# Feed-forward stage moved into the attentions' block: its first body runs among the attention's last products, its weights are rounded in six pieces, its buffers are lent

## The chip, the cores and the metric

One core of a Trainium2 chip runs the whole layer as one program. The metric is the device time of that program in microseconds (us); smaller is better. TensorE (PE) multiplies, VectorE (DVE) and ScalarE (ACT) work on tiles, GpSimd (POOL) does small vector work, SyncE (SP) issues the transfers. Each engine runs its own instructions in the order in which they are written; engines meet through semaphores.

## The reference, cut to what matters

Tokens are x of 32 batches by 64 positions by 256 features.

```python
x = x + attention1(mixture_of_experts(x, cond))          # 8 experts, top 2
def cond2(x, t):                                          # t is cond_256
    x = x + _attention(_tc_rmsnorm(x, t, g1w, g1b, b1w, b1b), Wq, Wk, Wv, Wo)
    return x + _swiglu(_tc_rmsnorm(x, t, g2w, g2b, b2w, b2b), gate_w, hid_w, out_w)
def _tc_rmsnorm(x, t, gw, gb, bw, bb):
    g = (t @ gw.T + gb)[:, None, :]; b = (t @ bw.T + bb)[:, None, :]
    return g * x * jax.lax.rsqrt(jnp.mean(x * x, axis=-1, keepdims=True) + 1e-6) + b
def _swiglu(x, gate_w, hid_w, out_w):                     # hidden width 1024
    return jax.nn.silu(x @ gate_w.T) * (x @ hid_w.T) @ out_w.T
x = x + slot_ffn(cond2(x, cond))                          # 16 slots with an expert each
```

The change concerns the second attention (`_attention` above) and `_swiglu`.

## The kernel before, in words

The program is a row of stages: `route`, `experts` with `routed_experts`, `attention` (both attentions, one after the other), `swiglu`, `slots` and the rest. A stage with its own `nc.Block()` ends in a barrier of all engines, and its semaphores are cleared there. `routed_experts` and `attention` share one block ("mid"), so attention starts while the last expert tiles finish. `swiglu` has its own block.

Tokens lie as 16 tiles of 128 (TT = 16), and work goes by bodies of two tiles, 256 tokens (NBODY = 8). `attention` runs the first attention's bodies 0 to 7 (tiles t = 0 to 15), then the second's (j = 0 to 7, t = 16 to 31), in an order written out by hand for each engine. A body of the second attention has `keys`, `queries` and `values` (12 matmuls of 256 columns each, since each product is made of three with operands split in a rounded high and a low part, `mm3`), and for each of its two tiles `scores`, `turn_weights` and `results`; `turn_results` and `project_results` of the body before are put between. On DVE a tile's `softmax` is a maximum and a subtraction over 1024 columns; `masked` writes the keys `kx` three times under a mask (`scores` of the next body waits for it); ACT does `exps`, the copies out of PSUM (`keys`, `queries`, `weights`, `results_turned`) and `squares` (the sums of squares for the next norm). The input of a body goes: `scaled` on ACT, `turn` on PE, `adapt` on DVE, `biased` on POOL, `high` on ACT, `low` on DVE.

The feed-forward stage's weights, 3 MB, are fetched into `g.w_ff` by SP in one transfer after the first attention's tile 0 (L805), in front of the transfers that the later bodies need (`results_in`, `load`). In `swiglu`, ACT takes a square root of all tokens' norms, rounds each of three weights whole (`wh`, 128x2048) and DVE makes the low parts (`wl`). Then eight bodies run, each with four steps j: `pair` (12 matmuls into pG, 12 into pH), ACT `silu` of pG, DVE `gated` (product with pH), ACT `hidden_high`, DVE low part, PE `output` (12 matmuls into pO). Body i's first `pair` goes ahead of the last `output` of body i - 1. Bodies 2 to 5 are a loop of two bodies' code, run twice. Beside these, `turn_key_weights`, `slot_queries`, `stationary`, `slot_scores_of_features` and `fold_high`/`fold_low` prepare folded weights for `slots`. SP stores `g.x1` to memory and loads weights of a later stage into `g.w_small` and `g.x1` (`lent_down`, `lent_up`).

Of the kernel before, what the change touches and what calls it, by code (L numbers as in the profile page):

```python
# [646 lines left out]

HD1 = DH + 1
# [52 lines left out]
def attention(nc, g, dr, block, sem):  # L701
    with ExitStack() as ctx:
# [8 lines left out]
        gat = [[sb(f"gat{c}{n}", [P, 2, D]) for n in range(2)] for c in range(2)]  # L711
        ya = [sb(f"ya{a}", [P, D]) for a in range(2)]
        yt = [sb(f"yt{a}", [P, D]) for a in range(2)]
        vst = [sb(f"vst{a}", [P, 4, 8, 2, HD1]) for a in range(2)]
        condT = sb("condT", [DC, NB])
        adaw = sb("adaw", [DC, 4, D])
        adab = sb("adab", [P, 4, KD])
        wh = [sb(f"wh{n}", [P, KD, D], F32R) for n in range(4)]
        wl = [sb(f"wl{n}", [P, KD, D], F32R) for n in range(4)]
        wo = sb("wo", [P, KD, D])  # L720
        neg = sb("neg", [P, 2])
        rows = [sb(f"rows{a}", [P, 2, D]) for a in range(2)]
        rT = sb("rT", [P, KD, PB])
        xb = [sb(f"xb{a}", [P, 2, D]) for a in range(2)]
        junk = [sb(f"junk{a}", [P, D]) for a in range(2)]
        xT = sb("xT", [P, KD, PB])
        kT = sb("kT", [P, KD, PB])
        m4 = sb("m4", [P, HR])
        warm = sb("warm", [P, HR])
# [6 lines left out]
        ol = sb("ol", [P, KD, PB], F32R)  # L736
        mx = [sb(f"mx{a}", [P, NH]) for a in range(2)]
# [3 lines left out]
        rs = [sb(f"rs{n}", [P, TT]) for n in range(4)]  # L741

# [6 lines left out]
        pR = pA[:, 0:NH * HD1].rearrange("p (h d) -> p h d", h=NH)  # L749
        pa = pD[:, 0:4 * KD * NB].rearrange("p (n k b) -> p n k b", n=4, k=KD)  # L750
# [8 lines left out]
        ada_in, ada_ps, ada_sb, ff_in, wo_in, neg_ok, rs_ok, inv_ok = (  # L759
            sem(n) for n in ("ada_in", "ada_ps", "ada_sb", "ff_in", "wo_in", "neg_ok", "rs_ok", "inv_ok"))  # L760
        wh_ok, wl_ok, u1_ok, u2_ok, uh_ok, ul_ok, q_ps, q_sb, ot_ps, oh_ok, ol_ok, o2_ps, o2_sb = (
            sem(n) for n in ("wh_ok", "wl_ok", "u1_ok", "u2_ok", "uh_ok", "ul_ok", "q_ps", "q_sb", "ot_ps", "oh_ok", "ol_ok", "o2_ps", "o2_sb"))
        o_out = [sem(f"o_out{a}") for a in range(2)]
# [6 lines left out]
        def _(sp):  # L770
# [42 lines left out]
        def _(pool):  # L813
# [25 lines left out]
            def biased(j):  # L839
                pool.wait_ge(u1_ok, j + 1)  # L840
                if j > 0:
                    pool.wait_ge(ul_ok, j)
                nc.gpsimd.tensor_tensor(batches(u2[:, :, :]), batches(u1[:, :, :]), bc(g.ada[:, 1, :, 4 * j:4 * j + 4], 3, S), ALU.add).then_inc(u2_ok, 1)
# [22 lines left out]
            for j in range(NBODY):  # L866
                if j < 4:
                    root(j + 4)
                if j + 2 < NBODY:
                    biased(j + 2)  # L870

        @block.tensor
        def _(pe):
            def turn(b):
# [4 lines left out]
                if b > NBODY:  # L879
                    pe.wait_ge(k_sb, 2 * b)  # L880
                    pe.wait_ge(u1_ok, b - NBODY)
# [136 lines left out]

            pe.wait_ge(ada_in, 48)
# [54 lines left out]
            for j in range(NBODY):  # L1074
                t = TT + 2 * j
                scores(t + 1)
                if j + 1 < NBODY:
                    keys(j + 1)
                turn_weights(t)
                if j + 1 < NBODY:  # L1080
                    queries(j + 1)
# [5 lines left out]
                if j + 1 < NBODY:  # L1087
                    scores(t + 2)
                if j + 2 < NBODY:
                    turn(NBODY + j + 2)  # L1090
# [5 lines left out]
                else:  # L1096
                    if j + 1 < NBODY:
                        values(j + 1)
# [4 lines left out]
            project_results(NBODY - 1)  # L1103

        @block.scalar
        def _(act):
# [15 lines left out]
            def scaled(j):  # L1122
                act.wait_ge(inv_ok, j + 1)
                act.wait_ge(x_ps, NBODY + j)
                for a in range(2):
                    nc.scalar.activation(yt[a][:, :], g.x1[:, 2 * j + a, :], ACT.Copy, scale=g.inv1[:, 2 * j + a:2 * j + a + 1]).then_inc(yt_ok, 1)
# [7 lines left out]
            def high(j):  # L1134
                act.wait_ge(u2_ok, j + 1)
                if j > 0:
                    act.wait_ge(q_ps, j)
                    act.wait_ge(v_ps, NBODY + j)
                nc.scalar.activation(uh[:, :, :], u2[:, :, :], ACT.Copy).then_inc(uh_ok, 1)
# [113 lines left out]
            for j in range(NBODY):  # L1253
                t = TT + 2 * j
                if j + 1 < NBODY:
                    keys(j + 1)
                weights(t)
                if j + 1 < NBODY:
                    queries(j + 1)
                if j > 0:  # L1260
                    results_turned(j - 1)
                if j + 2 < NBODY:
                    scaled(j + 2)
# [6 lines left out]
                if j + 1 < NBODY:  # L1270
                    exps(t + 2)
                    values(NBODY + j + 1)
# [4 lines left out]
            squares(N2 - 3)  # L1277
            squares(N2 - 2)
            results_turned(NBODY - 1)
            squares(N2 - 1)  # L1280

        @block.vector
        def _(dve):
# [15 lines left out]
            def adapt(j):  # L1299
# [3 lines left out]
                v.tensor_tensor(batches(u1[:, :, :]), batches(two(pC)), bc(g.ada[:, 0, :, 4 * j:4 * j + 4], 3, S), ALU.mult).then_inc(u1_ok, 1)  # L1303

            def low(j):
                dve.wait_ge(uh_ok, j + 1)
                v.tensor_tensor(ul[:, :, :], u2[:, :, :], f32(uh[:, :, :]), ALU.subtract).then_inc(ul_ok, 1)
# [83 lines left out]
            for j in range(NBODY):  # L1391
                t = TT + 2 * j
                softmax(t + 1)
                if j + 1 < NBODY:
                    masked(NBODY + j + 1)
# [3 lines left out]
                if j + 1 < NBODY:  # L1399
                    softmax(t + 2)  # L1400
                if j + 2 < NBODY:
                    adapt(j + 2)
                if j < LAG:
# [3 lines left out]
                    if j + 2 < NBODY:  # L1407
                        low(j + 2)
                else:
                    if j + 1 < NBODY:  # L1410
                        values(NBODY + j + 1)
# [9 lines left out]
def self_attention(nc, g, dr, first, w_raw, wo_raw, res, out, ssq):  # L1421
    if not first:
        with g.moe_sems, ExitStack() as ctx:
            _, _, sem = scope(nc, ctx, "mid")
            block = ctx.enter_context(nc.Block())
            routed_experts(nc, g, dr, block, sem)
            attention(nc, g, dr, block, sem)


def project_first(nc, g, dr):  # L1430

    pass


KF = FH // P
MP = KF // 2


def swiglu(nc, g, dr):
# [11 lines left out]
    with ExitStack() as ctx:  # L1451
        sb, ps, sem = scope(nc, ctx, "ffn")
        wh = [sb(f"wh{n}", [P, KD * FH], F32R) for n in range(3)]
        wl = [sb(f"wl{n}", [P, KD * FH], F32R) for n in range(3)]
        ms = sb("ms", [P, TT])
# [1173 lines left out]
```

## Time and profile before

| | |
|---|---|
| time, median of 3 runs | 962.15 us (956.14 to 964.59) |
| the profiled execution's own time | 968.49 us |
| its span, first to last instruction | 966.3 us |
| mean granted TensorE clock | 0.929 |
| busy: PE / DVE / ACT / POOL | 87% / 61% / 56% / 20% |
| PE's first feed-forward matmul | 597.75 us |
| last feed-forward result | 739.60 us |

All times of rows count from the span's start. The profiled execution is one run, 6.3 us over the median; differences worked out in it are carried over to the median.

### The profile page before, as it was taken

The numbers are of one execution on the slowest core, as the hardware profiler recorded it, in microseconds if no ns is written. First come the engines' busy times: TensorE is split into PE (matmuls) and PEld (weight loads), VectorE is DVE, ScalarE is ACT, GpSimd is POOL, SyncE is SP. The second block draws the span as 40 slices with busy tenths as digits, with TensorE's granted clock in tenths as the row PEclk, the third lists the DMA queues.
The fourth block names the chain that finished last, engine by engine and source line by source line (L and its number), as shares of the span: only waits on it lengthen the run. The fifth ranks groups of instructions, "written<-read, shape, count | busy, mean of one in ns | idle before, by whom it ended". The sixth has DMA issues, their size and how long they took to land. (4 is left out here: it accounts for less than half of the span.)

```text
span 966.3 us, 21254 instructions
## 1 busy us (share of the span) xinstructions
PE 839.9 (87%) x8416; PEld 729.8 (76%) x8416; DVE 585.5 (61%) x916; ACT 540.1 (56%) x990; POOL 198.0 (20%) x208
## 2 busy tenths in 40 slices
PE   6339989999999978899999985999998975977797
PEld 4239989999999975677778875999998973433354
DVE  3737766777777638788668754454443765321196
ACT  3219877888888735577576655433332541432364
POOL 0032444444354222235221000000000000000052
PEclk8559999999999999999999985999999996997899
DMA  8153666666666424542100005000002933999321
GB/s 327 45 218 125 220 224 215 239 246 233 232 230 230 138 92 144 109 89 45 35 2 1 3 1 218 1 1 1 0 1 106 422 117 165 399 423 425 129 85 67
DMA packets 70374, 145.04 MB, mean 150 GB/s; under 512 B 42648, under 2 KB 48280, under 8 KB 62728
## 3 DMA queue, kind: packets, MB, share of 16 engines
q1 hardware_dynamic: 63504, 127.25, 36.4%
q0 software_dynamic: 5168, 14.36, 4.5%
q10 hardware_dynamic: 1608, 2.12, 0.6%
q8 instruction: 65, 1.06, 0.4%
q14 instruction: 29, 0.24, 0.1%
HBM read 129.29 MB, written 14.42 MB: 149 GB/s over the span
## 5 line engine op out<-in xcount | busy, mean ns | idle before, releaser
L84 PE MATMUL moe_pH<-moe_hh,moew_wh 128*128 128x256 f32 x368 | 102.7, 279 | 0.9 <-DVE moe_hl L608 0.9
L85 PE MATMUL moe_pH<-moe_hh,moew_wl 128*128 128x256 f32 x368 | 102.5, 279 | 0.0
L86 PE MATMUL moe_pH<-moe_hl,moew_wh 128*128 128x256 f32 x368 | 102.5, 278 | 0.0
L608 DVE TENSOR_TENSOR moe_hl<-k_w_ff,moe_hh 128x512 fp32r<-128x512 f32 x92 | 63.8, 693 | 59.9 <-ACT moe_hh L570 59.9
L455 POOL DMA_INDIRECT results_of_experts<-k_w_ff,moew_place_of x46 | 67.5, 1468 | 152.0 <-DMA results_of_experts<-k_w_ff,moew_place_of 92.9
L561 ACT ACTIVATE k_w_ff<-moe_pH,moe_b 128x256 f32<-128x256 f32 x184 | 76.9, 469 | 29.2 <-PE moe_pH L86 29.2
L84 PEld LDWEIGHTS moe_pH<-moe_hh,moew_wh 128*128 128x128 f32 x368 | 69.8, 190 | 1.4 <-DVE moe_hl L608 1.1
L85 PEld LDWEIGHTS moe_pH<-moe_hh,moew_wl 128*128 128x128 f32 x368 | 69.1, 188 | 0.0
L86 PEld LDWEIGHTS moe_pH<-moe_hl,moew_wh 128*128 128x128 f32 x368 | 69.1, 188 | 0.0
L463 POOL DMA_INDIRECT k_w_ff<-in_x_tm,moew_row_of x46 | 52.3, 1137 | 73.8 <-POOLq L71 51.3
L570 ACT ACTIVATE moe_hh<-k_w_ff 128x512 fp32r<-128x512 f32 x92 | 58.2, 632 | 2.9
L599 DVE TENSOR_TENSOR moew_wl<-k_x,moew_wh 128x1024 fp32r<-128x1024 f32 x48 | 56.6, 1221 | 4.8 <-ACT moew_wh L546 3.6
L84 PE MATMUL moe_pY<-moew_wh,moe_hh 128*128 128x256 f32 x180 | 52.8, 293 | 1.6 <-DVE moe_hl L608 1.6
L599 DVE TENSOR_TENSOR moew_wl<-moew_raw,moew_wh 128x1024 fp32r<-128x1024 f32 x44 | 52.0, 1222 | 3.0 <-ACT moew_wh L546 2.7
L84 PE MATMUL moe_pH<-moe_xh,moew_wh 128*128 128x256 f32 x184 | 52.2, 284 | 1.5 <-DVE moe_xl L603 1.5
L1808 POOL DMA_DIRECT2D queries_of_tokens<-slots_qT x8 | 4.5, 561 | 235.1 <-ACT slots_qT L1913 235.1
L86 PE MATMUL moe_pH<-moe_xl,moew_wh 128*128 128x256 f32 x184 | 52.1, 283 | 0.0
L85 PE MATMUL moe_pH<-moe_xh,moew_wl 128*128 128x256 f32 x184 | 52.1, 283 | 0.0
L1688 DVE TENSOR_TENSOR ffn_hf<-ffn_pH,ffn_sg 128x512 f32<-128x512 f32 x32 | 22.1, 692 | 48.8 <-PE ffn_pH L86 35.6
L86 PE MATMUL moe_pY<-moew_wl,moe_hh 128*128 128x256 f32 x180 | 51.0, 283 | 0.0
L85 PE MATMUL moe_pY<-moew_wh,moe_hl 128*128 128x256 f32 x180 | 51.0, 283 | 0.0
L546 ACT ACTIVATE moew_wh<-k_x 128x1024 fp32r<-128x1024 f32 x44 | 45.2, 1051 | 8.9 <-PE moe_pY L86 6.2
(389 smaller groups left out, 2605.7 us busy)
## 6 DMA issues: line engine op xcount, KB each, us to landing
ring<-in_w_slot SPq DMA_DIRECT2D x10, 2048.0 KB, 17.5
k_x<-in_w SPq DMA_DIRECT2D x24, 512.0 KB, 6.6
k_x<-in_w SPq DMA_DIRECT2D x12, 1024.0 KB, 6.7
moew_raw<-in_w SPq DMA_DIRECT2D x22, 512.0 KB, 6.1
moew_raw<-in_w SPq DMA_DIRECT2D x11, 1024.0 KB, 6.6
ring<-in_w_slot SPq DMA_DIRECT2D x9, 1024.0 KB, 16.9
k_w_ff<-in_w_slot SPq DMA_DIRECT2D x4, 2048.0 KB, 11.8
attn_gat<-results_of_experts SPq DMA_DIRECT2D x16, 256.0 KB, 3.5
```

The costliest lines, as they stand in the source:

```text
L84: nc.tensor.matmul(out, ah, bh, start=start, stop=False)
L85: nc.tensor.matmul(out, al, bh, start=False, stop=False)
L86: return nc.tensor.matmul(out, ah, bl, start=False, stop=stop)
L455: nc.gpsimd.indirect_dma_start(out=dr.ys, out_offset=bass.IndirectOffsetOnAxis(ap=g.place_of[:, 2 * j + s:2 * j + s + 1], axis=0), in_=ys[ ...
L463: nc.gpsimd.indirect_dma_start(out=xr[j % 2][:, s, :], out_offset=None, in_=x_rows, in_offset=bass.IndirectOffsetOnAxis(ap=g.row_of[:, 2 * ...
L546: nc.scalar.activation(wh[a][l][:, n], raw_w[a][l][:, n], ACT.Copy).then_inc(wh_ok[l], 1)
L561: last = nc.scalar.activation(ht[l][:, 2 * i + m, :], pH[l][i][:, m, :], ACT.Relu, bias=b12[j % 2][:, l * KM + 2 * i + m:l * KM + 2 * i + ...
L570: nc.scalar.activation(hh[l][:, 2 * i:2 * i + 2, :], ht[l][:, 2 * i:2 * i + 2, :], ACT.Copy).then_inc(hh_ok[l], 1)
L599: v.tensor_tensor(wl[a][l][:, n], raw_w[a][l][:, n], f32(wh[a][l][:, n]), ALU.subtract).then_inc(wl_ok[l], 1)
L608: v.tensor_tensor(hl[l][:, s, :], ht[l][:, s, :], f32(hh[l][:, s, :]), ALU.subtract).then_inc(hl_ok[l], 1)
L1688: v.tensor_tensor(hf[j % 2][:, :, :], pH[j % 2][:, :, :], sg[j % 2][:, :, :], ALU.mult).then_inc(hf_ok, 1)
L1808: pool.dma_start(dr.q[i:i + 1].rearrange("o p k n -> p (o k) n"), qT[i % 2][:, :, :]).then_inc(q_out[i % 2], 16)
```

## The change

`swiglu` is emptied and its work put into `attention`, within the block "mid":

- `kx`, `df` and `ex` lie in `g.w_ff` (`lent`), which is therefore not loaded. The weights come in six pieces of 128x1024 (512 KB) into `raw`, two halves of `g.w_small`, during the second attention; SP issues them after the first attention's last output and the store of `g.x1`, each from the third on after the piece two before it is rounded.
- ACT's `feed_high` and DVE's `feed_low` round one piece at the end of each of the second attention's bodies j = 2 to 6, and the sixth in the last one. `feed_low` waits for `feed_high` of the same piece.
- The root of each feed-forward body's norm is taken on POOL (`second_root`, six small operations) and not on ACT.
- Bodies of the input chain run on: `scaled`, `turn`, `adapt`, `biased` (body 0) and `high`, `low` take the indices 8 to 15.
- The last attention body (t = 30, 31) is written out anew, with `gate`, `raised`, `lowered` (the former `pair` and `output`) of feed-forward body 0 between its products. pG and pH are halves of pS, pO is pD, and the split inputs and hidden values lie in `uh`, `ul`, `wh` and `wl`.
- The eight feed-forward bodies are unrolled. `turn_key_weights` moves behind body 0, `slot_scores_of_features` into body 1, the folds into body 2.
- One barrier (between attention and feed-forward) is gone; the one left clears the semaphores of both.

```diff
-        kx = sb("kx", [P, KD, HR, PB])
-        df = [sb(f"df{a}", [P, NH, S]) for a in range(2)]
-        ex = [sb(f"ex{a}", [P, NH, S]) for a in range(2)]
+        lent = g.w_ff[:, :, :].rearrange("p n m -> p (n m)")
+        kx = lent[:, 0:2048].rearrange("p (k r n) -> p k r n", k=KD, r=HR)
+        df = [lent[:, 2048 + 1024 * a:3072 + 1024 * a].rearrange("p (h k) -> p h k", h=NH) for a in range(2)]
+        ex = [lent[:, 4096 + 1024 * a:5120 + 1024 * a].rearrange("p (h k) -> p h k", h=NH) for a in range(2)]
...
+        fh = [sb(f"fh{n}", [P, KD * FH], F32R) for n in range(3)]
+        fl = [sb(f"fl{n}", [P, KD * FH], F32R) for n in range(3)]
+        raw = [g.w_small[:, 2 - 2 * n:4 - 2 * n].rearrange("p w k n -> p (w k n)") for n in range(2)]
+        ih, il = (uh, wh[0]), (ul, wl[0])
+        hh, hl = (wh[1], wh[2]), (wl[1], wl[2])
+        sg = [lent[:, 512 * r:512 * r + 512].rearrange("p (m n) -> p m n", m=2) for r in range(2)]
+        hf = [lent[:, 1024 + 512 * r:1536 + 512 * r].rearrange("p (m n) -> p m n", m=2) for r in range(2)]
...
-                if t == 0:
-                    sp.dma_start(g.w_ff[:, :, :], dr.w_ff).then_inc(ff_in, 16)
                 if t % 2 == 0 and t >= 2:
                     load(t // 2 - 1)
             load(NBODY - 1)
-            sp.wait_ge(ff_in, 16)
+            sp.dma_start(slotT[:, :, :], dr.slotT).then_inc(sl_in, 16)
+            sp.wait_ge(wl_ok, 3)
+            sp.wait_ge(o1_sb, NBODY)
+            sp.dma_start(g.x1_home, g.x1[:, :, :]).then_inc(x1_out, 16)
+            for p in range(6):
+                if p >= 2:
+                    sp.wait_ge(fl_ok, p - 1)
+                sp.dma_start(raw[p % 2], dr.w_ff[:, p // 2, p % 2 * FH:(p % 2 + 1) * FH]).then_inc(raw_in[p % 2], 16)
+            sp.wait_ge(fl_ok, 6)
+            sp.dma_start(g.lent_down[0], dr.w_slot[LENT, :, W2_AT:W_SLOT]).then_inc(g.lent_down_in[0], 16)
...
+            def second_root(i):
+                c = slice(2 * i, 2 * i + 2)
+                pool.wait_ge(sq_ok, 2 * (NBODY + i) + 2)
+                nc.gpsimd.tensor_scalar(ms[:, c], g.ss2[:, c], 1.0 / D, EPS, ALU.mult, ALU.add).then_inc(rs2_ok, 1)
...
+                elif j < NBODY - 1:
+                    second_root(j - 4)
+                if j + 2 <= NBODY:
                     biased(j + 2)
+            for i in range(NBODY - 5, NBODY):
+                second_root(i)
...
+            def gate(i, j):
+                n = MP * i + j
+                if j == 0:
+                    pe.wait_ge(uh_ok, NBODY + i + 1)
+                    pe.wait_ge(ul_ok, NBODY + i + 1)
+                if n == 0:
+                    pe.wait_ge(fh_ok, 2)
+                    pe.wait_ge(fl_ok, 2)
+                if n < 2:
+                    pe.wait_ge(df_ok, 2 * TT - 1)
+                else:
+                    pe.wait_ge(sg_ok, n - 1)
+                features_of(pG[j % 2], 0, i, j).then_inc(g_ps, 1)
...
+            t = 2 * TT - 2
+            scores(t + 1)
+            turn_weights(t)
+            turn_results(NBODY - 2)
+            results(t)
+            gate(0, 0)
+            turn_weights(t + 1)
+            raised(0, 0)
+            results(t + 1)
+            project_results(NBODY - 2)
+            gate(0, 1)
+            raised(0, 1)
             turn_results(NBODY - 1)
+            lowered(0, 0)
             project_results(NBODY - 1)
+            turn(N2 + 1)
+            for j in range(2, MP):
+                gate(0, j)
+                raised(0, j)
+                lowered(0, j - 1)
+            turn_key_weights()
...
+            def feed_high(n, half):
+                act.wait_ge(raw_in[half], 16 * (n + 1))
+                c = slice(half * FH, (half + 1) * FH)
+                nc.scalar.activation(fh[n][:, c], raw[half], ACT.Copy).then_inc(fh_ok, 1)
...
+                if j >= 2:
+                    feed_high((j - 2) // 2, j % 2)
+            high(NBODY)
+            t = 2 * TT - 2
+            weights(t)
+            exps(t + 1)
+            results_turned(NBODY - 2)
+            squares(N2 - LAG - 2)
+            feed_high(2, 1)
+            silu(0, 0)
+            weights(t + 1)
+            squares(N2 - LAG - 1)
+            scaled(NBODY + 1)
+            silu(0, 1)
+            hidden_high(0, 0)
             squares(N2 - 2)
             results_turned(NBODY - 1)
+            hidden_high(0, 1)
+            high(NBODY + 1)
             squares(N2 - 1)
+            for j in range(2, MP):
+                silu(0, j)
+                hidden_high(0, j)
+                if j == 2:
+                    scaled(NBODY + 2)
...
+            def feed_low(n, half):
+                dve.wait_ge(fh_ok, 2 * n + half + 1)
+                c = slice(half * FH, (half + 1) * FH)
+                v.tensor_tensor(fl[n][:, c], raw[half], f32(fh[n][:, c]), ALU.subtract).then_inc(fl_ok, 1)
...
+                if j >= 2:
+                    feed_low((j - 2) // 2, j % 2)
+            t = 2 * TT - 2
+            softmax(t + 1)
+            low(NBODY)
+            results(t)
+            output_low(NBODY - 2)
+            feed_low(2, 1)
+            results(t + 1)
+            second_output(NBODY - 2)
+            gated(0, 0)
             output_low(NBODY - 1)
+            gated_low(0, 0)
+            gated(0, 1)
+            gated_low(0, 1)
             second_output(NBODY - 1)
+            adapt(NBODY + 1)
+            gated(0, 2)
+            gated_low(0, 2)
+            low(NBODY + 1)
+            gated(0, 3)
+            gated_low(0, 3)
```

## Rows read from the trace of the kernel before

**Rows 1.** Windows: busy time and count per engine, PE clock, DMA share, GB/s.

```profile
540.00:560.00 20.00, 19.52 (x252) 17.01 (x244) 15.30 (x26) 14.97 (x33) 1.04 (x1) 1.00 0.01 2
...
580.00:600.00 20.00, 9.10 (x42) 8.55 (x43) 8.45 (x11) 12.67 (x23) 0.00 (x0) 0.56 0.54 208
...
572.00:574.00 2.00, 1.79 (x8) 1.42 (x8) 0.00 (x0) 0.69 (x2) 0.00 (x0) 0.56 0.00 0
```

**Rows 2.** Timeline, attention's end to the slots' start: start, duration, work, idle before, releaser.

```profile
588.36 1.28 ACT L1652 ACT_TABLE_LOAD   x1 [1.65 <-PEq L71]
...
597.75 0.55 PE L84 MATMUL ffn_pG<-ffn_ih,ffn_wh 128*128 128x256 f32 x1 [3.40 <-DVE ffn_il L1680]
...
599.66 1.28 ACT L1619 ACT_TABLE_LOAD   x1
600.96 0.60 ACT L1619 ACTIVATE ffn_sg<-ffn_pG 128x512 f32<-128x512 f32 x1
...
607.42 0.28 PE L1580 MATMUL ffn_pO<-ffn_wl,ffn_hh 128*128 128x256 f32 x1
...
739.60 0.69 DVE L1695 TENSOR_TENSOR k_x<-ffn_pO,k_x 128x512 f32<-128x512 f32 x1 [1.84 <-PE ffn_pO L1580]
...
741.21 0.63 PE L1819 MATMUL slots_pX<-k_ident,k_x 128*128 128x128 f32 x4 [1.65 <-PEq L71]
```

**Rows 3.** Timeline of PE: the score products of the second attention.

```profile
546.62 1.09 PE L665 MATMUL attn_pS<-attn_kx,attn_qT 64*64 64x256 f32 x16
...
553.23 1.09 PE L665 MATMUL attn_pS<-attn_kx,attn_qT 64*64 64x256 f32 x16
...
560.12 1.09 PE L665 MATMUL attn_pS<-attn_kx,attn_qT 64*64 64x256 f32 x16
```

**Rows 4.** Timeline of DVE and ACT in the same body.

```profile
547.79 1.23 DVE L1328 TENSOR_REDUCE attn_mx<-attn_pS 128x16 f32<-128x1024 f32 x1 [0.17 <-PE attn_pS L665]
...
553.92 0.68 DVE L1356 TENSOR_TENSOR k_x<-attn_pB,k_x 128x512 f32<-128x512 f32 x1
...
556.91 1.27 DVE L1314 TENSOR_SCALAR attn_kx<-attn_kT,attn_m 128x512 f32<-128x512 f32 x3
559.80 0.69 DVE L1352 TENSOR_TENSOR attn_ol<-attn_pB,attn_oh 128x512 fp32r<-128x512 f32 x1 [1.62 <-ACT attn_oh L1202]
...
552.02 0.63 ACT L1139 ACTIVATE attn_uh<-attn_u 128x512 fp32r<-128x512 f32 x1 [2.16 <-POOL attn_u L843]
...
555.18 0.19 ACT L1211 ACTIVATION_READ_ACCUMULATOR attn_junk<-k_x 128x1 f32 x1
```

**Rows 5.** The page's costliest groups: busy us, mean ns of one, idle before.

```profile
L599 DVE TENSOR_TENSOR moew_wl<-k_x,moew_wh 128x1024 fp32r<-128x1024 f32 x48 | 56.6, 1221 | 4.8 <-ACT moew_wh L546 3.6
...
L1688 DVE TENSOR_TENSOR ffn_hf<-ffn_pH,ffn_sg 128x512 f32<-128x512 f32 x32 | 22.1, 692 | 48.8 <-PE ffn_pH L86 35.6
...
L546 ACT ACTIVATE moew_wh<-k_x 128x1024 fp32r<-128x1024 f32 x44 | 45.2, 1051 | 8.9 <-PE moe_pY L86 6.2
```

**Rows 6.** Timeline of PE in the last attention body: its waits.

```profile
569.32 0.63 PE L1003 MATMUL attn_pB<-k_ident,attn_otm 128*128 128x128 f32 x4 [0.83 <-ACT attn_pt L1184]
...
572.08 0.94 PE L962 MATMUL attn_pA<-k_ident,attn_ex 128*128 128x128 f32 x4 [1.07 <-DVE attn_otm L1343]
...
582.30 0.39 PE L84 MATMUL attn_pB<-attn_wh,attn_oh 128*128 128x256 f32 x1 [1.52 <-DVE attn_ol L1352]
```

**Rows 7.** First attention: the weights' transfer (KB, us to landing), then PE's timeline.

```profile
k_w_ff<-in_w_ff SPq DMA_DIRECT2D x1, 3072.0 KB, 10.6
...
390.91 0.75 PE L884 MATMUL attn_pC<-k_ident,attn_yt 128*128 128x128 f32 x4 [2.11 <-DVE attn_yt L1297]
391.59 1.99 PE L665 MATMUL attn_pS<-attn_kx,attn_kT 64*64 64x256 f32 x16
...
404.48 0.66 PE L884 MATMUL attn_pC<-k_ident,attn_yt 128*128 128x128 f32 x4
...
416.46 0.66 PE L884 MATMUL attn_pC<-k_ident,attn_yt 128*128 128x128 f32 x4
```

More of the change, by code:

```diff
@@ new lines, in turn_key_weights @@
+            def turn_key_weights():
+                pe.wait_ge(ot_ok, 2 * TT)
+                pe.wait_ge(o2_sb, NBODY)
+                for c in range(KD):
+                    for k in range(KD):
+                        last = nc.tensor.transpose(two(pA)[:, c, k * P:(k + 1) * P], g.w_small[:, W_DK, k, c * P:(c + 1) * P], g.ident[:, :])
+                last.then_inc(wk_ps, 1)
+                pe.wait_ge(sl_in, 16)
+                for m in range(KD):
+                    for k in range(KD):
+                        last = nc.tensor.matmul(pB[:, m * NS:(m + 1) * NS], g.w_small[:, W_DQ, k, m * P:(m + 1) * P], slotT[:, k, :], start=k == 0, stop=k == KD - 1)
+                last.then_inc(sq_ps, 1)
@@ L1073, in _ @@
             values(0)
-            for j in range(NBODY):
+            for j in range(NBODY - 1):
                 t = TT + 2 * j
                 scores(t + 1)
-                if j + 1 < NBODY:
-                    keys(j + 1)
+                keys(j + 1)
                 turn_weights(t)
-                if j + 1 < NBODY:
-                    queries(j + 1)
+                queries(j + 1)
                 if j > 0:
@@ L1096, in _ @@
                 else:
-                    if j + 1 < NBODY:
-                        values(j + 1)
+                    values(j + 1)
                     results(t + 1)
@@ L1398, in _ @@
                 results(t)
[L1399 to L1402, printed above, removed]
+                softmax(t + 2)
+                adapt(j + 2)
                 if j < LAG:
@@ L1416, in _, with kept @@
                     second_output(j - 1)
+                if j >= 2:
[9 more added lines that the diff above has]
+            gated(0, 0)
             output_low(NBODY - 1)
+            gated_low(0, 0)
+            gated(0, 1)
+            gated_low(0, 1)
             second_output(NBODY - 1)
[L1421 to L1439, printed above, removed]
+            adapt(NBODY + 1)
[4 more added lines that the diff above has]
+            gated_low(0, 3)
+            for i in range(1, NBODY):
+                gated(i, 0)
+                gated_low(i, 0)
+                fed(i - 1)
+                if i + 1 < NBODY:
+                    adapt(NBODY + i + 1)
+                gated(i, 1)
+                gated_low(i, 1)
+                if i == 1:
+                    stationary()
+                gated(i, 2)
+                gated_low(i, 2)
+                if i + 1 < NBODY:
+                    low(NBODY + i + 1)
+                gated(i, 3)
+                gated_low(i, 3)
+                if i == 2:
+                    for n in range(3):
+                        fold_low(n)
+            fed(NBODY - 1)
+def kept(nc, g, dr):
     g.more, g.fold = ExitStack(), ExitStack()
@@ L1741, with self_attention, project_first, swiglu @@
+def self_attention(nc, g, dr, first, w_raw, wo_raw, res, out, ssq):
+    if not first:
+        with g.moe_sems, ExitStack() as ctx:
+            _, _, sem = scope(nc, ctx, "mid")
+            block = ctx.enter_context(nc.Block())
+            routed_experts(nc, g, dr, block, sem)
+            kept(nc, g, dr)
+            attention(nc, g, dr, block, sem)
+def project_first(nc, g, dr):
+    pass
+def swiglu(nc, g, dr):
+    pass
 NRING = 4
```

499 lines of the change are left out of this document (198 added, 301 removed).

## The prediction, made before the changed kernel was run

> **What bounds the kernel now.** I read the windows first, to see where each engine is full, then the timelines of the stretch around the change, and last the first attention, because a transfer leaves it. In the second attention PE is full (19.5 of 20 us) while DVE has 15.3 and ACT 15.0; between 580 and 600 us PE has 9.1 us and a clock of 0.56 [rows 1]. A body of the second attention takes 560.12 - 546.62 = 13.50 us [rows 3]: PE sets it. The feed-forward stage is PE's alone as well: from the end of body 0's first `output` at 607.5 to the last result at 739.6 it needs 132.1 us [rows 2] for 1092 of its 1152 large matmuls, 0.121 us each with the small work between. What is not PE's is the joint. The last two attention bodies' products wait on ACT and DVE [rows 6], the clock falls to half at 572 [rows 1], then come the barrier, the table load for the root, the rounding of weights, and the first product starts only at 597.75, still slow (0.55 us against 0.28 later) [rows 2]. The change aims at this joint.
>
> **The change, part by part.** I count from the score product at 553.23 [rows 3], which opens the last body but one's second half, to the last feed-forward result at 739.60 [rows 2]: 186.4 us before. After, this stretch is the following sum.
>
> 1. One full attention body, 13.5 us [rows 3]. Before, this body (j = 6) lacked `turn`, `adapt`, `biased` and `high`; now it has them for feed-forward body 0.
>
> 2. The last body's attention products at full clock, about 9.3 us: 13.5, less `keys`, `queries`, `values` (36 matmuls at 0.121, 4.4), less one score product (1.0) and one `turn` (0.6), plus one more `turn_results` (0.6) and `project_results` (12 x 0.121, 1.5), less the 0.4 us of waits in a body.
>
> 3. The whole feed-forward stage at its own rate: 132.1 x 1152 / 1092 = 139.4 us. Same order of products, same copies, so I keep the rate; the code is unrolled now, as the attention's code is already, where PE shows no wait for instructions. `turn_key_weights` lies inside it now: 0.9 us at full clock.
>
> 4. The pieces. One costs ACT 1.05 and DVE 1.22 us [rows 5]. Both have idle time in a body, but they work in order and this is where I expect the price. `feed_low` is queued on DVE ahead of the next `softmax`, and waits for ACT, which comes to `feed_high` only after `squares`. Behind it on DVE stand `softmax`, `masked` and all else, and for `masked` the next `scores` on PE waits. I follow the ring: DVE's maximum at 547.79 leads by way of `adapt` and POOL to ACT's `high` at 552.02; ACT ends `squares` at 555.4; `feed_high` to 556.3, `feed_low` to 557.5. In the profile the next maximum begins right behind the result of 553.92 + 0.68 and the masks end at 556.91 + 1.27 = 558.2 [rows 4], 3.6 us later; so now they end at 561.1. The score product of 1.09 us follows and the ring closes with the next maximum at 562.4. That is 14.6 us in place of 13.50, and 1.15 us for each piece. Four pieces (j = 2 to 5) delay a following body: 4.6 us. Bounds: nothing, if the slack of rows 4 (DVE 1.62 us) took it; 2.3 us each, if both roundings came in series, 9.2. I take the ring's value since each of its links is a row.
>
> 5. Waits of PE in the last body. `turn_results` waits for ACT's `weights`, which now stand behind `high` and the fifth piece, about 1.0; `gate(0, 0)` waits for DVE's `softmax` of the last tile (late by the fifth piece) and `low`, 1.0; `results` of the last tile waits for `weights`, which ACT does after the sixth piece (1.05), a table load of 1.28 and the first `silu` of 0.60 [rows 2, 5], 1.9; `lowered(0, 0)` waits for `turn_results`, ACT's copy, `output_low` and `gated_low` at 0.69 each [rows 4, 5], 2.1. Sum 6.0. Before, the nearest waits there were 0.83, 1.07 and 1.52 [rows 6], 3.4 together, which is my lower end; the upper is 10, if each grew by another piece. Behind a late `weights` nothing but this same chain stands.
>
> 6. The clock. Waits of about 1 us in this very place were followed by half clock at 572 [rows 1, 6], a wait of 2.11 by two score products' time (1.99 for 1.09) [rows 7]. With gate products between, one dip is likely: half clock for some 4 us costs 2.0. Ends 0 and 5.
>
> 7. The exit. The barrier with the attention's semaphores took 1.65 us, the one after feed-forward 0.9 (740.3 to 741.2) [rows 2]; the larger stands at the end now: 0.7.
>
> Sum: 13.5 + 9.3 + 139.4 + 0.9 + 4.6 + 6.0 + 2.0 + 0.7 = 176.4 us, 10.0 less than 186.4. The root's table load, the three whole roundings and the first barrier are gone in this; they were in front of 597.75 and nothing takes their place, since `second_root` runs on POOL, which has 1 us of work in 20 [rows 1], and a body ahead of its use.
>
> 8. The first attention. The 3 MB transfer takes 10.6 us to land, and `results_in` is queued behind it; PE waits 2.11 us for that input and then runs its score product at 1.99 us. The body from 390.91 to 404.48 is 13.57 us where the next is 11.98 [rows 7]. Without the transfer I take back the part of the wait that the neighbouring body doesn't have, 1.4, and the 1.6 us: 3.0 (0 to 3.7). The pieces come later, when the DMA engines are at 0.01 [rows 1]: six of 512 KB, by the 3 MB in 10.6 us under 3 us each, a body or two ahead of their use. The store of `g.x1` ahead of them (2 MB) has a body as well. `lent_down` and `lent_up` still end a hundred us before `slots`. No cost.
>
> So 13.0 us less. The profiled execution's own 968.49 becomes 955.5; against the median of the runs, 6.3 lower, 962.15 becomes 949.1, and I say 949.
>
> ACT now has three `squares` between `silu`s (in the last attention body), and no row shows whether the two share a table: `squares` between exponentials need no load, a root does (1.28 us) [rows 2]. If not, ACT gets four more loads, 5.1 us, of which those ahead of `results_turned` and the third `silu`, about 2 us, would reach PE.
>
> The Trainium skill, page "ScalarE: Activation LUTs", section "What ACT_TABLE_LOAD costs", has a higher price: about 2.66 us for each switch, drain included. Here `silu` starts 1.30 us after its load begins, so the trace disagrees as far as the wait is seen; by the page the four loads would be 10.6 us. The section "Table sets: the hidden batching unit" of the same page says that cheap functions are in every set as filler, without naming the square.
>
> **The rivals.**
>
> A. The pieces' waits pull down the clock in each body. PE would sit 1 us more before `scores` in five bodies. For it: half clock after the waits of rows 6 and 7. Against it: a body full of large matmuls lies around the wait. The dip after 390.91 cost 1.6 us (step 8), five of them 8.0: 5.0 us faster only, 957.1.
>
> B. Slower than before: the same place, worse. The pieces are in series (2.3 us a body, 1.15 more than I take, 4 times, 4.6) and each of the five bodies has two such dips, 16.0. Then 20.6 - 13.0 is 7.6 us slower, 969.7. It decides from 2.6 us a body on. Against it: in rows 1 PE keeps full clock in this stage.
>
> C. The overlap doesn't come: the last body's chain (scores, exponentials, results, projection) is so stretched by the inserted ACT and DVE work that feed-forward body 0 is only moved around in it. Waits of 10 us and a clock loss of 5 in place of 8 leave 6.0 us, 956.2.
>
> D. Table loads at each `squares`: 2 us less, 951.1.
>
> **How the numbers follow.** A difference within 1% (9.6 us) can hardly be told from none here. Forecast 0.58, A 0.16, B 0.05, C 0.15, D 0.06. The range for 8 in 10 reaches to A and C and to the good ends of steps 4 to 6 (4.6 + 2.6 + 2.0, of which I take most): 941 to 960. Faster by over 1% (below 952.5) is the forecast and D without their upper part: 0.61; slower by over 1% is part of B: 0.04; the rest, 0.35, is within 1%.
>
> **What would show it.** Score products 14.6 us apart from body 3 on, with DVE idle before the low part of a piece on ACT (step 4; 13.5 would mean it is free). Bodies 2 and 3 of the first attention at 11 to 12 us (step 8). First gate product about 6 us after the last score product, and PE waits of 6 us until `lowered(0, 0)` (step 5). Clock 1.0 in the second attention (against A, B). Feed-forward bodies at 17.1 us as before (step 3). One table load around the squares (D). I am wrong if the feed-forward bodies are slower unrolled or if the last attention body costs PE over 16 us of waiting.

## The result and the profile after

The changed kernel takes 956.5 us (median of 20 runs, 947.8 to 965.5); the kernel before took 963.2 us beside it (20 runs). The ratio is 0.992 (0.990 to 0.995): 7.4 us faster, give or take 2.5, where I had forecast 13.0. That is under 1%, but the interval does not reach 1, so the change is faster by a little. The ratio is formed over all fast executions, so its 7.4 us are not the 6.7 between the medians. The changed kernel's profiled execution took 956.16 us, span 954.3, clock 0.946. The one before took 968.49, 5 us over its own median and slower than 19 of the 20 timed runs, so the two profiles differ by 12.3 us and not by 7.4. That alone warns against reading one against the other to the microsecond.

Windows of the changed kernel, as [rows 1]:

```profile
540.00:560.00 20.00, 17.99 (x233) 15.95 (x231) 15.59 (x23) 15.43 (x31) 6.24 (x13) 1.00 0.18 53
560.00:580.00 20.00, 16.16 (x219) 14.10 (x216) 14.39 (x24) 15.58 (x33) 7.05 (x15) 1.00 0.13 40
580.00:600.00 20.00, 17.94 (x154) 17.73 (x153) 9.39 (x15) 7.59 (x19) 4.96 (x17) 1.00 0.32 122
```

The hole of [rows 1] is gone: between 580 and 600 us PE has 17.9 us of work at a clock of 1.00, where it had 9.1 at 0.56. But the attention's bodies, which had PE at 19.5 of 20, now have 18.0. PE's timeline shows the score products, as [rows 3], and then every wait of the last body, as [rows 6]:

```profile
546.31 1.09 PE L667 MATMUL attn_pS<-k_w_ff,attn_qT 64*64 64x256 f32 x16 [0.77 <-issue]
...
552.86 1.09 PE L667 MATMUL attn_pS<-k_w_ff,attn_qT 64*64 64x256 f32 x16
...
560.92 1.09 PE L667 MATMUL attn_pS<-k_w_ff,attn_qT 64*64 64x256 f32 x16 [0.76 <-issue]
...
567.47 1.10 PE L667 MATMUL attn_pS<-k_w_ff,attn_qT 64*64 64x256 f32 x16
...
570.42 0.63 PE L1055 MATMUL attn_pB<-k_ident,attn_otm 128*128 128x128 f32 x4 [0.83 <-ACT attn_pt L1380]
...
572.71 0.36 PE L84 MATMUL attn_pS<-attn_uh,attn_fh 128*128 128x256 f32 x1 [0.60 <-issue]
...
578.27 1.13 PE L690 MATMUL attn_pA<-attn_vst,attn_pt 128*64 128x34 f32 x32 [1.65 <-ACT attn_pt L1380]
...
586.33 0.36 PE L1121 MATMUL attn_pD<-attn_fh,attn_wh 128*128 128x256 f32 x1 [2.06 <-issue]
```

A body now takes 560.92 - 546.31 = 14.61 us instead of 13.50. The waits sum to 0.83 + 0.60 + 1.65 + 2.06 = 5.14 us. The ring of the piece, on ACT and DVE, as [rows 4]:

```profile
554.94 1.04 ACT L1309 ACTIVATE attn_fh<-k_w_small 128x1024 fp32r<-128x1024 f32 x1
...
553.60 0.68 DVE L1620 TENSOR_TENSOR k_x<-attn_pB,k_x 128x512 f32<-128x512 f32 x1
556.01 1.23 DVE L1543 TENSOR_TENSOR attn_fl<-k_w_small,attn_fh 128x1024 fp32r<-128x1024 f32 x1 [1.74 <-ACT attn_fh L1309]
557.16 1.22 DVE L1592 TENSOR_REDUCE attn_mx<-attn_pS 128x16 f32<-128x1024 f32 x1
...
559.55 1.27 DVE L1578 TENSOR_SCALAR k_w_ff<-attn_kT,attn_m 128x512 f32<-128x512 f32 x3
```

DVE stands idle 1.74 us for `feed_high`, and the maximum of the next tile, whose product had long been done, begins only behind `feed_low`. The masks end at 560.82 and the score product starts at 560.92. The end of the stage, as [rows 2], and ACT's only table load in the joint:

```profile
575.35 1.28 ACT L1316 ACT_TABLE_LOAD   x1
576.64 0.60 ACT L1316 ACTIVATE k_w_ff<-attn_pS 128x512 f32<-128x512 f32 x1
577.13 0.59 ACT L1380 ACTIVATE attn_pt<-attn_pA 128x512 f32<-128x512 f32 x1
...
578.09 0.43 ACT L1407 ACTIVATE attn_junk<-k_x 128x256 f32<-128x256 f32 x1
```

```profile
724.74 0.69 DVE L1561 TENSOR_TENSOR k_x<-attn_pD,k_x 128x512 f32<-128x512 f32 x1 [1.82 <-PE attn_pD L1123]
...
727.46 0.63 PE L1832 MATMUL slots_pX<-k_ident,k_x 128*128 128x128 f32 x4 [2.76 <-PEq L71]
```

The weights for `turn_weights` of the last tile (577.13) stand behind the load and the first `silu`. The squares at 578.09 follow a `silu` without another load. Last, the first attention, as [rows 7]:

```profile
375.83 0.66 PE L936 MATMUL attn_pC<-k_ident,attn_yt 128*128 128x128 f32 x4 [0.57 <-DVE attn_yt L1522]
376.42 1.99 PE L667 MATMUL attn_pS<-k_w_ff,attn_kT 64*64 64x256 f32 x16
...
388.99 0.66 PE L936 MATMUL attn_pC<-k_ident,attn_yt 128*128 128x128 f32 x4 [0.60 <-DVE attn_yt L1522]
389.58 1.09 PE L667 MATMUL attn_pS<-k_w_ff,attn_kT 64*64 64x256 f32 x16
```

The wait of 2.11 us is down to 0.60. The slow score product (1.99 us) is still there, a body earlier; in both repeats of this kernel below it is not (see step 8).

### The profile page after: what moved, and what is told of

It reads as the page before. It is cut to its first block and busy times, and to the rows that moved or that the text cites. A ratio compares the mean times of both kernels' runs of the same rounds, so it can differ in the third digit from the quotient of the medians.

```text
span 954.3 us, 21191 instructions
## 1 busy us (share of the span) xinstructions
PE 837.6 (88%) x8416; PEld 728.9 (76%) x8416; DVE 584.2 (61%) x916; ACT 537.7 (56%) x991; POOL 214.8 (23%) x257
## 5 line engine op out<-in xcount | busy, mean ns | idle before, releaser
L463 POOL DMA_INDIRECT k_w_ff<-in_x_tm,moew_row_of x46 | 48.5, 1053 | 76.2 <-POOLq L71 53.9
L1551 DVE TENSOR_TENSOR k_w_ff<-attn_pS,k_w_ff 128x512 f32<-128x512 f32 x32 | 22.1, 691 | 50.4 <-PE attn_pS L86 34.6
L546 ACT ACTIVATE moew_wh<-moew_raw 128x1024 fp32r<-128x1024 f32 x44 | 45.1, 1051 | 6.4 <-DMA moew_raw<-in_w 3.9
```

The lines of the kernel that those rows point to most:

```text
L463: nc.gpsimd.indirect_dma_start(out=xr[j % 2][:, s, :], out_offset=None, in_=x_rows, in_offset=bass.IndirectOffsetOnAxis(ap=g.row_of[:, 2 * ...
L546: nc.scalar.activation(wh[a][l][:, n], raw_w[a][l][:, n], ACT.Copy).then_inc(wh_ok[l], 1)
L1551: v.tensor_tensor(hf[j % 2], pH[j % 2], sg[j % 2], ALU.mult).then_inc(hf_ok, 1)
```

## The experiments

All were timed against the kernel before on their own chip. Beside each median stands a length read from the profile: from the start of the score product of tile 23 (508.99 in the changed kernel, just ahead of the first body that a piece delays) to the end of the last `lowered` matmul. It holds all delays by pieces, the joint and the whole feed-forward stage, and leaves out the other stages, whose time varies in unaltered code too: the first and the third profile of the changed kernel have spans of 954.3 and 946.2 us, and this stretch takes 215.7 in both.

| kernel | median us | ratio to before (95%) | stretch us |
|---|---|---|---|
| before | 963 to 966 | 1 | 226.8 |
| e4_before_late_ff | 961.4 | 0.998 (0.995 to 1.001) | 224.1 |
| changed, three times | 956.5, 956.5, 957.7 | 0.992, 0.992, 0.992 (0.988 to 0.996) | 215.7, 218.6, 215.7 |
| e7_exit_only | 954.9 | 0.990 (0.987 to 0.993) | 218.5 |
| e5_not_among, twice | 953.7, 957.3 | 0.990, 0.992 (0.985 to 0.996) | 221.3, 221.4 |
| e1_low_later | 948.9 | 0.984 (0.979 to 0.988) | 211.5 |
| e2_tail_order | 947.8 | 0.982 (0.977 to 0.986) | 212.0 |
| e3_both | 949.0 | 0.983 (0.978 to 0.988) | 208.1 |
| e6_exit, twice | 946.1, 946.5 | 0.981, 0.980 (0.976 to 0.983) | 208.0, 208.0 |
| e8_apart_rest_mended | 953.2 | 0.987 (0.984 to 0.991) | 214.0 |

**The base.** The changed kernel again, unaltered, twice.

> The changed kernel again, unaltered, on the chip that runs the next three: the base that they are compared with. Both theories: about 956.5 us, 5 to 10 us below the kernel before. If the profiled clock of the last 230 us is below 1.00 here, the tail of the earlier profile was a lucky one.

> The changed kernel, unaltered, on the chip of this batch: about 956 us. With it e5_not_among_again is judged on one chip.

956.5 and 957.7 us. The stretch was 218.6 us the first time, 2.9 more than in the first profile, and 215.7 the second. The difference is clock alone. PE's timeline of the first repeat:

```profile
556.82 1.98 PE L667 MATMUL attn_pS<-k_w_ff,attn_qT 64*64 64x256 f32 x16 [0.76 <-issue]
564.96 1.09 PE L667 MATMUL attn_pS<-k_w_ff,attn_qT 64*64 64x256 f32 x16
...
578.79 0.41 PE L84 MATMUL attn_pS<-attn_uh,attn_fh 128*128 128x256 f32 x1
```

A score product at half clock behind a piece's wait of 0.76 us costs 1.6 us in the half body. From there on the clock is full again until 577.2, behind the wait for `results` (1.62 us here), where it is half a second time, over projection and gate products. I call each such stretch, at a granted clock of 0.50, a dip. e7_exit_only, whose code is the same there, shows it again; the other two profiles do not. So two of four executions of this code lose 2.8 to 2.9 us here. Three more profiles of the table have the same code up to this product, with the same wait of 0.76 us: both profiles of e5_not_among show the slow product (1.98 and 1.99 us) and e2_tail_order's does not. The five profiles in which the next experiment's edit has taken this wait away (e1, e3, e6 twice, e8) all have it at 1.09 us. So this first dip comes in four of seven executions with the wait and in none of five without it; and the second comes in those two of the four executions that have the first.

**Where a piece's price comes from.**

```diff
                 masked(NBODY + j + 1)
+                if j >= 3:
+                    feed_low((j - 3) // 2, (j - 1) % 2)
                 if j > 0:
                     output_low(j - 1)
...
-                if j >= 2:
-                    feed_low((j - 2) // 2, j % 2)
```

> One edit: on VectorE the low part of a weight piece goes behind the next body's masks instead of ahead of its maximum; piece 5's low part lands in the last body beside piece 6's. Theory (the price of a piece is VectorE standing in order behind ScalarE's high part): score products return from 14.6 to 13.5 to 13.7 us apart, 4.0 to 4.5 us are gained on the changed kernel, of which up to 1 us may come back as a longer wait at the last results. Rival (the two engines' load itself closes the ring, wherever the piece stands): bodies stay at 14.3 us or more and the time is within 1 us of the changed kernel.

PE's and DVE's timelines of this kernel:

```profile
546.22 1.09 PE L667 MATMUL attn_pS<-k_w_ff,attn_qT 64*64 64x256 f32 x16
...
560.02 1.09 PE L667 MATMUL attn_pS<-k_w_ff,attn_qT 64*64 64x256 f32 x16
```

```profile
547.57 1.22 DVE L1592 TENSOR_REDUCE attn_mx<-attn_pS 128x16 f32<-128x1024 f32 x1
...
551.22 1.22 DVE L1543 TENSOR_TENSOR attn_fl<-k_w_small,attn_fh 128x1024 fp32r<-128x1024 f32 x1
553.15 0.69 DVE L1616 TENSOR_TENSOR attn_ol<-attn_pB,attn_oh 128x512 fp32r<-128x512 f32 x1 [0.72 <-ACT attn_oh L1398]
```

Bodies of 13.80 us, 0.81 of the 1.11 us a piece gone. The same two instructions per piece are there, now in DVE's idle time ahead of `output_low`. The stretch is 4.2 us shorter (215.7 to 211.5). So 0.81 us of the price was the order on DVE, as the theory says; the bodies stayed 0.10 us above the 13.7 that I had expected at most. By the medians it is 7.5 us, of which the dip described above, gone in this kernel, can be a part. The remaining 0.30 us a body lies at ACT: PE's timeline has, before `turn_results`, first here and then in the kernel before,

```profile
551.86 0.63 PE L1055 MATMUL attn_pB<-k_ident,attn_otm 128*128 128x128 f32 x4 [0.64 <-ACT attn_pt L1380]
```

```profile
558.51 0.63 PE L1003 MATMUL attn_pB<-k_ident,attn_otm 128*128 128x128 f32 x4 [0.24 <-ACT attn_pt L1184]
```

This wait for ACT's `weights` is 0.40 us longer (the rest of the body is 0.10 shorter), and `feed_high` stands ahead of `weights` in ACT's order. No run moved `feed_high`, so that it is the cause is not shown.

**The last body's order.**

```diff
+            weights(t + 1)
             feed_high(2, 1)
             silu(0, 0)
-            weights(t + 1)
...
             gated(0, 0)
-            output_low(NBODY - 1)
             gated_low(0, 0)
+            output_low(NBODY - 1)
```

> Only the order in the last attention body: on ScalarE the last tile's weights go ahead of the sixth piece, the table load and the first silu; on VectorE the first low part of the gated features goes ahead of the last body's output rounding. Theory (these two orders make the waits of 1.65 us before the last results and 2.06 us before the first lowered product): both waits fall below 0.5 us and 2.5 to 3.5 us are gained. Rival (other work, the silu chain or the last output's rounding, comes late next): the waits only move and less than 1 us is gained.

> The two edits together. Theory: they are in different bodies and add, 6.5 to 8 us gained on the changed kernel, 12 to 16 us on the kernel before. Rival: the fifth piece, now in the last body, takes the room that the second edit makes, and the sum is 2 us or more short of the two single gains.

The stretch falls by 3.7 us with this edit alone and by 7.6 with both, nearly the sum of 4.2 and 3.7, so they add. Against the kernel before the two make 17 us by the medians, where I had expected 12 to 16. Both of the large waits are as good as gone; what PE's timeline of e6_exit (same orders) shows in the place of the four waits is

```profile
564.90 0.63 PE L1055 MATMUL attn_pB<-k_ident,attn_otm 128*128 128x128 f32 x4 [0.83 <-ACT attn_pt L1380]
...
570.37 1.13 PE L690 MATMUL attn_pA<-attn_vst,attn_pt 128*64 128x34 f32 x32
...
576.48 0.36 PE L1121 MATMUL attn_pD<-attn_fh,attn_wh 128*128 128x256 f32 x1 [0.18 <-issue]
```

By medians each edit alone gives 8 us, and both together no more than one (949.0 against 948.9 and 947.8). The intervals, 5 us to either side for six runs, hold both readings, and the rest of e3_both's profile (from the last `lowered` to the end 232.5 us against 227.9 in e2) has code that no edit touches. I go by the stretch, and that the two edits add is shown by it alone.

**Is it the interleaving?** Body 0's products behind the attention's last ones, with ACT's and DVE's orders to match:

```diff
             results(t)
-            gate(0, 0)
             turn_weights(t + 1)
-            raised(0, 0)
             results(t + 1)
             project_results(NBODY - 2)
-            gate(0, 1)
-            raised(0, 1)
             turn_results(NBODY - 1)
-            lowered(0, 0)
             project_results(NBODY - 1)
+            gate(0, 0)
...
```

> The changed kernel with feed-forward body 0's first products behind the attention's last ones instead of among them; the shared block, the pieces and the lent buffers stay. Theory (the interleaving fills waits of PE in the last body, and the block without a barrier and the pieces bring the rest): PE waits 8 to 10 us between the last score product and the first lowered product instead of 5.1, and the time is 3 to 5 us above the changed kernel. Rival (the interleaving is worth all of the gain): 7 us or more above it, level with the kernel before.

> The kernel of e5_not_among again. Its first profile had the same waits in the last attention bodies as the kernel before (4.98 us) where the changed kernel has 5.14, so net of the clock the theory now says: within 1 us of the changed kernel, up to 3 above it by its dip. Rival (the first median was lucky): 4 us or more above it.

Both times the ratio is that of the changed kernel (0.990 and 0.992 against 0.992). Neither the expectation (PE waiting 8 to 10 us, 3 to 5 us slower) nor its rival (level with the kernel before) came true the first time; the second time the expectation, within 1 us of the changed kernel, did. PE's timeline:

```profile
563.97 0.63 PE L1055 MATMUL attn_pB<-k_ident,attn_otm 128*128 128x128 f32 x4 [0.83 <-ACT attn_pt L1380]
...
566.72 1.09 PE L1014 MATMUL attn_pA<-k_ident,k_w_ff 128*128 128x128 f32 x4 [1.06 <-DVE attn_otm L1607]
...
569.57 1.93 PE L690 MATMUL attn_pA<-attn_vst,attn_pt 128*64 128x34 f32 x32 [0.69 <-ACT attn_pt L1380]
...
574.85 0.63 PE L1055 MATMUL attn_pB<-k_ident,attn_otm 128*128 128x128 f32 x4 [0.88 <-DVE k_x L1620]
...
577.00 0.55 PE L84 MATMUL attn_pB<-attn_wh,attn_oh 128*128 128x256 f32 x1 [1.52 <-DVE attn_ol L1616]
...
579.69 0.41 PE L84 MATMUL attn_pS<-attn_uh,attn_fh 128*128 128x256 f32 x1
```

The five waits sum to 4.98 us, as in the kernel before, where they sum to 4.99 ([rows 6] has three of the five). The changed kernel has 5.14: with its interleaving PE has four waits in place of five, and the same sum. (The kernel without it has `weights` of the last tile ahead of the sixth piece on ACT, which the changed kernel has not; so this compares an interleaving that is badly fed with none that is fed well.) The first gate product comes 18.7 us after the last score product, without a wait of its own; before it took 31.4 (566.38 to 597.75). So most of the gain over the kernel before is the closed joint, not the overlap. By the stretch, 221.3 is 2.7 us over the changed kernel's profile with a dip and 5.6 over those without; both profiles without the interleaving have that dip themselves, so 2.7 is the difference of like with like. As the waits are nearly equal, it is clock: 0.75 between 560 and 580 us here, 0.93 there (e0_after). The medians (0.4 us apart on one chip) don't show even that, and each has an interval of 3 us; whether 3 us are lost is open.

The same question, with the other costs mended:

> The last run's e6_exit without the interleaving: low parts later, the shorter exit, and feed-forward body 0 behind the attention's last products. Theory (put among them in the order of e2_tail_order, body 0 fills the waits and keeps the clock up; put behind them, PE waits about 5 us as the kernel before did and drops to half clock): 4 to 8 us above e6_exit, the stretch from the last but fourteenth microsecond of attention scores to the last lowered result 172 to 175 us against its 166.6. Rival (waits hidden or not, the time is set elsewhere, as e5_not_among's level median could be read): within 2 us of e6_exit.

> The best version so far again, 946 us; the theory wants 4 to 8 us between it and e8_apart_rest_mended, and 8 to 11 us between it and the changed kernel.

Here it shows. 953.2 against 946.5 us on one chip, 214.0 against 208.0 in the stretch (172.5 against 166.6 from the score product of tile 29 on). The windows from 560 to 580 us, first of e8_apart_rest_mended, then of e6_exit:

```profile
560.00:580.00 20.00, 15.01 (x167) 13.02 (x164) 10.98 (x17) 13.17 (x33) 9.03 (x25) 0.91 0.21 62
```

```profile
560.00:580.00 20.00, 18.99 (x222) 17.51 (x219) 13.38 (x21) 15.26 (x36) 9.29 (x25) 1.00 0.16 54
```

PE is busy 19.0 of 20 us at full clock with the products among the attention's and 15.0 at 0.91 without. Its waits in the last body sum to 5.00 us without (0.83, 0.91, 0.69, 1.05, 1.52) and to 1.01 with (0.83, 0.18), which is 4.0 of the 6.0 us; the rest goes with the clock. Interleaving is worth 6 us once ACT and DVE serve it in the order in which PE asks. Against the changed kernel on the same chip e6_exit gains 11.2 us, just over the 8 to 11 expected. At 946 us twice, it is the best version found: 2% under the kernel before and 1% under the changed one.

**The exit.**

```diff
-    _, _, sem = scope(nc, g.moe_sems, "moew")
+    sem = g.sem
```

> Both orders of the run e3_both, and the expert stage's semaphores taken from the program's own scope, so that the exit ahead of the slots has one round of clearing and barrier less. Theory (the 1.1 us that the exit grew by is that second round, since the experts' semaphores are given back there too): PE's wait before the slots falls from 2.76 to about 1.65 us and half clock behind it gets shorter, 1 to 2.5 us gained on e3_both, about 946.5 us. Rival (the growth comes from the number of semaphores in one scope): the wait stays above 2.4 us and nothing is gained.

> The changed kernel with only the exit edit of e6_exit. Theory: PE's wait before the slots 1.65 us instead of 2.76, 1 to 2.5 us gained on the changed kernel, about 955 us. Rival: wait above 2.4 us, nothing gained.

PE's timeline of e6_exit, at the first product of the slots:

```profile
717.02 0.63 PE L1833 MATMUL slots_pX<-k_ident,k_x 128*128 128x128 f32 x4 [2.29 <-PEq L71]
```

The wait is 2.29 us in both kernels, from 2.76: the second round of clearing and barrier is 0.47 us, under half of the 1.1 that the exit grew by. Both bounds (1.65, 2.4) were off, and the other 0.64 us is open. In the medians it can't be seen: 1.6 to 2.8 us on different chips for e7, 2.9 for e6 over e3_both, all within the intervals.

**The transfer of step 8.** The kernel before, with this alone:

```diff
-                if t == 0:
-                    sp.dma_start(g.w_ff[:, :, :], dr.w_ff).then_inc(ff_in, 16)
...
             load(NBODY - 1)
+            sp.dma_start(g.w_ff[:, :, :], dr.w_ff).then_inc(ff_in, 16)
```

> The kernel before with one edit: the 3 MB transfer of the raw feed-forward weights is issued after the last input of the first attention instead of near its start. Theory of the prediction's step 8 (the transfer makes PE wait for its input and lose its clock): the body at 390.91 shrinks from 13.57 to about 12 us and 3.0 us are gained. Rival, from the changed kernel's trace (that body's wait and half clock only turn up one body earlier): 0 to 1 us.

2.4 us by the medians, 1.6 by the ratio, give or take 3: inconclusive between the two. PE's timeline says more:

```profile
368.52 0.80 PE L883 MATMUL attn_pC<-k_ident,attn_yt 128*128 128x128 f32 x4 [0.69 <-DVE attn_yt L1296]
369.24 1.99 PE L665 MATMUL attn_pS<-attn_kx,attn_kT 64*64 64x256 f32 x16
...
381.62 0.66 PE L883 MATMUL attn_pC<-k_ident,attn_yt 128*128 128x128 f32 x4 [0.60 <-DVE attn_yt L1296]
382.21 1.72 PE L665 MATMUL attn_pS<-attn_kx,attn_kT 64*64 64x256 f32 x16
```

The wait is down to 0.60 as in the changed kernel, and two score products run slow instead of one, so the body from this `turn` to the next takes 13.63 us (381.62 to 395.25) and not the 12 expected. From `turn(1)` of this attention (363.66 before) to the score product of tile 22 the kernel before takes 142.5 us at a mean clock of 0.98, this one 143.0 at 0.96, and the changed kernel 141.4 at 0.97 and 139.5 at 0.99. The wait went; whether the clock comes with it differs from execution to execution. The first repeat of the changed kernel (e0_after) has, at the same two score products,

```profile
373.89 1.09 PE L667 MATMUL attn_pS<-k_w_ff,attn_kT 64*64 64x256 f32 x16
...
385.42 1.09 PE L667 MATMUL attn_pS<-k_w_ff,attn_kT 64*64 64x256 f32 x16
```

Twelve profiles have the changed kernel's code in this stretch. Four have neither product slow and take 139.5 to 139.6 us, six have one slow and take 140.6 to 141.7, two have both and take 142.3 and 142.8. Their mean is 140.8.

This kernel has the joint of the kernel before unaltered, and needs 183.6 us from tile 29's score product to the last result's product, where the profile before needed 186.3. The waits are the same within 0.05 us; the difference is the clock again, 0.95 against 0.93: the half clock that the kernel before has from 572 to 579 us ([rows 1]) does not come here.

## Why the prediction was right in its mechanism and too high in its size

**Steps 1 to 7** took 10.0 us off, 10.7 without the exit. The pieces' delays lie ahead of tile 29 as well, so the stretch to hold this against is the table's: 226.8 - 10.7 = 216.1 us forecast, and 215.7, 218.6 and 215.7 measured. These agree within 2.5 us, in part because errors cancel. Part by part:

- Step 2: its terms sum to 9.2 and not 9.3; nothing hangs on it.
- Step 4, the pieces: 14.6 us forecast, 14.61 measured, by the ring forecast (masks ending 3.6 us behind the maximum), in the four bodies named. e1_low_later shows the cause.
- Step 5, waits: 6.0 forecast, 5.14 measured. `turn_results` 0.83 for 1.0, the gate 0.60 for 1.0, `results` 1.65 for 1.9, `lowered` 2.06 for 2.1. The lower end of 3.4 was read from three waits of the kernel before, which had five, 4.99 together. e2_tail_order shows the two large ones to be the orders of ACT and DVE.
- Step 6, clock: 2.0 forecast as one likely dip; two dips, 2.8 to 2.9 us together, in two of four executions and none in the others, 1.4 on average.
- Step 7, exit: 0.7 forecast, 1.1 measured (1.61 to 2.72 from the last result on). I had counted one barrier; the experts' semaphores are cleared in a second round there. That round is 0.47 us; the other 0.64 are open.
- Step 3, the stage at its own rate: undersized, which I had named as a sign of being wrong. A body takes (710.13 - 623.29) / 5 = 17.37 us; before, (725.19 - 639.54) / 5 = 17.13. Over the stage this is 1.7 us. That unrolling is the reason isn't shown: in the kernel before, the written-out bodies run at the loop's rate. The results of the changed kernel, then those of the kernel before, on DVE:

```profile
623.29 0.68 DVE L1561 TENSOR_TENSOR k_x<-attn_pD,k_x 128x512 f32<-128x512 f32 x1
...
710.13 0.68 DVE L1561 TENSOR_TENSOR k_x<-attn_pD,k_x 128x512 f32<-128x512 f32 x1
```

```profile
639.54 0.68 DVE L1695 TENSOR_TENSOR k_x<-ffn_pO,k_x 128x512 f32 x1
...
725.19 0.69 DVE L1695 TENSOR_TENSOR k_x<-ffn_pO,k_x 128x512 f32<-128x512 f32 x1
```

**Step 8** is the step whose reason failed: 3.0 us forecast, for a wait and for a slow product behind it. The wait's part came in every profile (2.11 to 0.60). The clock's part came only in some: from the 142.5 us of the kernel before, the stretch fell by 1.0 us in the first profile of the changed kernel, by 2.9 in both repeats, and by 1.7 in the mean of the twelve. I took a slow score product behind a long wait for a cost of that wait. e4_before_late_ff and eight of the twelve profiles keep such products behind waits of 0.6 to 0.8 us. The forecast's sign, bodies 2 and 3 of the first attention at 11 to 12 us, is met by both repeats (11.53 and 11.99 us in e0_after) and missed by the first profile (13.16 and 11.99).

**The carrying over to the median** failed too. I subtracted 13.0 us from an execution that was slow among its like, and whose joint took 186.3 us where e4's took 183.6 for the same code. If e4's is the usual one, which two executions can't show, then 2.7 us could not be saved from a median execution. The balance of the forecast's excess, with this taken so: 2.7 here, 1.3 in step 8, 1.7 in step 3, 0.4 in step 7, less 0.9 in step 5 and 0.6 in step 6, makes 4.6 of the 5.6 us between 13.0 and 7.4. It is an account from single profiles, and not a measurement of the 5.6.

So the mechanism of steps 4 and 5 was right and is shown. That 956.5 lies within 941 to 960 is in part luck: the range reached that far for rivals A and C, whose mechanisms did not occur, and not for the steps that were off. To an outcome within 1% I had given 0.35, to one faster by more 0.61.

**The rivals.** A (a dip at every body's wait) didn't come: the clock is 1.00 from 540 to 560 us, and where dips come, only one of the four bodies with a piece's wait has one (the second is behind `results`). B falls with it. C named 956.2 us, the time measured, but by a price that isn't there (waits of 10 us and 5 of clock); its thought, that body 0 is only moved around in the last body's chain, is nevertheless near to what e5_not_among shows, at waits of 5.14 us for 4.98 and 2.7 us of clock. D (loads at the squares) didn't come: one load at 575.35 and none at 578.09. The Trainium skill, page "ScalarE: Activation LUTs", section "What ACT_TABLE_LOAD costs", gives 2.66 us for a switch, drain included; here `silu` begins 1.29 us behind the start of its load (1.30 in [rows 2]), so the trace shows less than half of that.

## What to carry to other kernels

Work put among a stage's last products fills its waits only if the engines that feed both take their instructions in the order in which PE asks for them; otherwise it exchanges waits for waits, and closing the joint is most of the gain (here all but 2.7 us). Put the half of a two-engine job that waits for the other engine behind what the ring needs next, not ahead of it: the same instructions cost 1.11 us a body in one place and 0.30 in the other. And before subtracting a saving from a profile, ask whether the stretch that it closes was as long in that execution as it usually is.

## What was not expected of the hardware

- Identical code loses the half clock in some executions and not in others (215.7, 218.6 and 215.7 us for one stretch), behind waits of 0.76 us that were the same each time. A wait shows where a dip may come, not that it will: here in four of seven executions, and in none of the five in which the wait was gone.
- In the kernel before, groups of twelve 128x256 matmuls took 1.36 and 1.42 us by turns, in the code that loops and in the code that is written out; in the changed kernel all take 1.39 to 1.42 (the first group of a body, which takes longer in both, left out). It is the 0.24 us a body of step 3. No run here tells why.
- Squares and copies between `silu`s need no table load: behind the one at 575.35 ACT has no other until 733.99 us, when the stage is over.
